# A cross-network kernel (CIN) with x1 split by one instruction per chunk into two buffers, and 31 rounded fields in the last layer

## The chip, the cores and the metric

The kernel runs on one core of a Trainium2 chip. The metric is device time in microseconds, from the first to the last instruction with what lies around it. Engines are named as in the profile: PE is TensorE (matmuls; PEld is its weight load), DVE is VectorE, ACT is ScalarE, POOL is GpSimd, SP is SyncE, which here only issues DMAs.

## The reference

512 samples, 39 embedded fields of 16 dimensions. Three "cross" layers, whose outputs are summed over the 16 dimensions, and a small MLP behind them:

```python
def _cin_layer(X0, Xi, W, b):          # X0: [512, 39, 16], Xi: [512, fields, 16]
    Wr = W.reshape(H, F0_, Fi)
    return jnp.einsum('hjk,bjd,bkd->bhd', Wr, X0, Xi) + b[None, :, None]
Xi = X0
for W, b in Ws:                        # 3 layers of 128 outputs each
    Xi = _cin_layer(X0, Xi, W, b)
    res.append(Xi.sum(axis=2))
z = jnp.concatenate(res, axis=1)       # [512, 384]
h = jnp.concatenate([z, dense_ctx], axis=1)
h = jnp.maximum(h @ W_top1 + b_top1, 0.0)
h = jnp.maximum(h @ W_top2 + b_top2, 0.0)
y = h @ W_top3
```

## The kernel before

**Tiling.** The 512 samples go through in 16 chunks of 32 samples, so a chunk is 512 columns (sample times dimension), and a chunk in 4 groups of 128 columns. Rows of the tables are gathered by GpSimd three chunks ahead, laid out by a transpose, written to a scratch in DRAM and read back in the layouts that the layers need.

**Layer 0** of the next chunk is 7 fp32 matmuls (`layer0`, L409) into the PSUM bank `acc0`, each on a product that GpSimd makes (`multiply0`, L259). They are spread through the current chunk by a list written by hand (`L0_AFTER`, L75), the last one behind block 1 of group 3. Then `evacuate_x1` (L655, ScalarE) writes `x1` = `acc0` + bias. The columns of `acc0` are interleaved by group, so the read steps over four fp32 values at a time, and `x1` lies group after group.

**Layer 1** needs `x1` as two values that the fast matmul form (fp32r, 3 matmuls for one product) takes: `x1h`, `x1` rounded by a ScalarE copy, and `x1l` = `x1` - `x1h`, by VectorE. There is one buffer of each. To let the next chunk's values be written while group 3 of the old one is still being used, both are made in two pieces: FRONT, the 384 columns of groups 0 to 2 (ScalarE L662, VectorE L577 by `split_x1`), and BACK, the 128 columns of group 3 (ScalarE L667 in `split_back`, VectorE L577), which is made early in the chunk itself, once the last matmuls of the old chunk are through. TensorE waits for the first at group 0 (L445) and for the second at group 3 (L447).

A group of layer 1 is 10 blocks (`layer1_block`, L424) of 3 matmuls L436 to L438, 4 fields (512 columns) to a block. Each block's output is multiplied with `x0t` and summed by its owner, `OWNERS = "ADADAADADA"` (L59): six blocks go to ScalarE (banks `ya`, four), which scales them into `prods`, and four (numbers 1, 3, 6 and 8) to VectorE (banks `yd`, two), which chains multiply-adds (L558). VectorE also adds up `prods` in two halves per group (`sum_half`, L561, L573) into `x2t`. TensorE may write block 3 of a group into its `yd` bank only when VectorE is through with block 8 of the group before.

**Order on VectorE at the turn between chunks** (`chunk`, L585): multiply-adds of block 6 of group 3; FRONT of the next x1; the sum of half 0; the multiply-adds of block 8; then in the next chunk those of block 1; BACK; the sum of half 1, on which the `gram_group` matmul (L416) waits; block 3. One chunk later in the order, at group 1, `sum_dims` (L580) sums `x1` over the dimensions. Chunks 1 to 14 are a hardware loop on VectorE and chunks 1 to 13 on ScalarE; TensorE's are written out.

**Last layer** (L505): 39 fields of `w2` times `gram` into one bank. The first `whole` = 12 fields are plain fp32 matmuls (L509); the last `split` = 27 take three fp32r matmuls each (L514 to L518). For these, `w2` is split into the space of `w1h`/`w1l` (23 fields) and then of `x1h`/`x1l` (4 fields, 512 columns) by ScalarE L729 and VectorE L627, and each field of `gram` by ScalarE L735 and VectorE L632, through a ring of four. ScalarE evacuates the last `gram` group (L671) behind its two `w2` pieces.

Of the kernel before, what the change touches and what calls it, by code (L numbers as in the profile page):

```python
# [119 lines left out]
def build(nc, a):  # L120
    ctx = ExitStack()
    with ctx:
        def sb(name, shape, dt=F32):
            return ctx.enter_context(nc.sbuf_tensor(name, shape, dt))
# [4 lines left out]
        def sem(name):  # L129
            return ctx.enter_context(nc.semaphore(name))  # L130
# [17 lines left out]
        x1h = sb("x1h", [P, COLS], F32R)  # L148
        x1l = sb("x1l", [P, COLS], F32R)
# [6 lines left out]
        z = sb("z", [P, 2, B])  # L156
# [20 lines left out]
        split = near + COLS // H  # L177
        whole = F - split

        def w2_halves(i):  # L180
# [4 lines left out]
            return x1h[:, cols], x1l[:, cols]  # L185
# [5 lines left out]
        def w2_pieces():  # L191

            rows = w2[:, whole:F, :].rearrange("p j h -> p (j h)")
            return ((rows[:, 0:near * H], w1h[:, first_split * H:], w1l[:, first_split * H:]),
                    (rows[:, near * H:], x1h[:, :], x1l[:, :]))

        h1, h2 = gram[:, 0:4, :], gram[:, 4:6, :]
# [25 lines left out]
        x1h_front, x1h_back = sem("x1h_front"), sem("x1h_back")  # L223
        x1_front, x1_back = sem("x1_front"), sem("x1_back")
# [8 lines left out]

        FRONT, BACK = slice(0, (GROUPS - 1) * P), slice((GROUPS - 1) * P, COLS)
# [39 lines left out]
        def _(sp):  # L274
# [48 lines left out]
            sp.wait_ge(x1_back, CHUNKS)  # L323
# [69 lines left out]
        def _(pe):  # L393
# [30 lines left out]
            def layer1_block(n, g, q):  # L424
# [12 lines left out]
                pe.matmul(out, x1h[:, xs], w1l[:, cols], start=False, stop=False)  # L437
                pe.matmul(out, x1l[:, xs], w1h[:, cols], start=False, stop=True).then_inc(ready, 1)  # L438

            def chunk(c, prev, nxt, lay):  # L440

                l0_after = L0_AFTER if prev else L0_AFTER_0
                for g in range(GROUPS):
                    if g == 0:
                        pe.wait_ge(x1_front, c + 1)  # L445
                    if g == GROUPS - 1:
                        pe.wait_ge(x1_back, c + 1)  # L447
                    for q in range(BLOCKS):
                        layer1_block(GROUPS * c + g, g, q)
# [39 lines left out]
            def hidden1_early(m):  # L489
                pe.matmul(hid[m][:, :], wt1_0[:, m * P:(m + 1) * P], z[:, 0, :], start=True, stop=False)  # L490
# [33 lines left out]
            for m, out in enumerate(hid):  # L524
                pe.matmul(out[:, :], wt1[:, 1, m * P:(m + 1) * P], z[:, 1, :],
                          start=False, stop=True).then_inc(tail_mm, 1)
# [14 lines left out]
        def _(dve):  # L541
# [33 lines left out]
            def split_x1(c, cols, high, done):  # L575
                dve.wait_ge(high, c + 1)
                dve.tensor_tensor(x1l[:, cols], x1[:, cols], x1h[:, cols].bitcast(F32),  # L577
                                  ALU.subtract).then_inc(done, 1)

            def sum_dims(c):  # L580
                dve.tensor_reduce(z[:, 0, bass.ds(c * CB, CB)].rearrange("p (g b) -> p g b", g=GROUPS),
                                  x1[:, :].rearrange("p (g d b) -> p g b d", g=GROUPS, d=D), AX.X,
                                  ALU.add).then_inc(z_sums, 1)
# [34 lines left out]
            split_x1(0, FRONT, x1h_front, x1_front)  # L618
# [16 lines left out]
        def _(act):  # L635
# [19 lines left out]
            def evacuate_x1(c):  # L655
# [31 lines left out]
            def chunk(c, prev, nxt, lay):  # L687
                split_back(c)
# [50 lines left out]
            act.activation(z[:, 1, :], yd[0][:, :], ACT.Identity, bias=bias2d[:, 0:1]).then_inc(tail_act, 1)  # L739
# [74 lines left out]
```

## Time and profile before

| what | value |
|---|---|
| median of 3 runs | 677.56 us (677.14 to 682.29) |
| the profiled execution | 677.52 us |
| its span, first to last instruction | 675.7 us |
| TensorE, busy share | 95% |
| VectorE, busy share | 85% |
| ScalarE, busy share | 76% |
| GpSimd, busy share | 51% |

Busy time of TensorE is a union of pipelined matmuls whose ends are modelled: a 512-column fp32r matmul is shown with 0.39 us, but one starts every 0.227 us. So the distance between starts is what is read on TensorE, and a gap shows as a start that comes later than that. The same holds in part for VectorE and ScalarE, where the next instruction may start a little before the shown end of the one before.

### The profile page before, as it was taken

The numbers are of one execution on the slowest core, as the hardware profiler recorded it, in microseconds if no ns is written. First come the engines' busy times: TensorE is split into PE (matmuls) and PEld (weight loads), VectorE is DVE, ScalarE is ACT, GpSimd is POOL, SyncE is SP. The second block draws the span as 40 slices with busy tenths as digits, with TensorE's granted clock in tenths as the row PEclk, the third lists the DMA queues.
The fourth block names the chain that finished last, engine by engine and source line by source line (L and its number), as shares of the span: only waits on it lengthen the run. The fifth ranks groups of instructions, "written<-read, shape, count | busy, mean of one in ns | idle before, by whom it ended". The sixth has DMA issues, their size and how long they took to land.

```text
span 675.7 us, 13663 instructions
## 1 busy us (share of the span) xinstructions
PE 639.8 (95%) x2489; PEld 457.9 (68%) x2489; DVE 577.4 (85%) x1240; ACT 514.3 (76%) x1676; POOL 346.7 (51%) x339
## 2 busy tenths in 40 slices
PE   0389999999999999999999999999999999999998
PEld 0166677677777777777777777777777777766473
DVE  0457898989899999989998989999999989999580
ACT  2156878888787878787878878787878887899372
POOL 6778384838474665647383847475563333220000
PEclk9989999999999999999999999999999999999999
DMA  6532723232231303131323222231313130000200
GB/s 220 137 101 57 242 65 90 53 88 53 63 78 49 93 22 91 32 97 44 88 53 89 52 73 68 56 85 30 86 29 105 31 102 16 13 16 2 62 1 0
DMA packets 42542, 46.12 MB, mean 68 GB/s; under 512 B 20704, under 2 KB 25408, under 8 KB 42377
## 3 DMA queue, kind: packets, MB, share of 16 engines
q1 hardware_dynamic: 26146, 42.28, 21.3%
q0 software_dynamic: 5120, 1.32, 2.1%
q10 hardware_dynamic: 11239, 2.05, 1.7%
q8 instruction: 20, 0.33, 0.2%
q14 instruction: 17, 0.14, 0.1%
HBM read 44.30 MB, written 1.31 MB: 68 GB/s over the span
## 4 chain that ended last, share of the span: by engine, by line
PE 82%; POOL 4%; DVE 4%; issue 4%; DMA 3%; SPq 1%; ACT 1%; DVEq 0%; ACTq 0%; POOLq 0%
PE acc L413 14%; PE ya L436 11%; PE ya L437 11%; PE ya L438 10%; PE yd L436 8%; PE yd L438 7%; PE yd L437 7%; PE misc L420 4%; POOL emb L339 3%; DVE chain L558 2%; DMA tiles<-x_rows 2%; PE yd L509 2%; POOL prod L266 1%; PE yd L514 1%; PE yd L518 1%
## 5 line engine op out<-in xcount | busy, mean ns | idle before, releaser
L683 ACT ACTIVATE prods<-ya,x0t 128x128 f32<-128x128 f32 x1472 | 442.5, 501 | 100.5 <-PE ya L438 100.1
L558 DVE SCALAR_TENSOR_TENSOR chain<-yd,x0t,chain 128x128 f32<-128x128 f32 x768 | 218.2, 343 | 14.4 <-PE yd L438 13.7
L436 PE MATMUL ya<-w1h,x1h 128*128 128x512 f32 (+1 forms) x384 | 206.4, 537 | 1.9 <-DVE x1l L577 1.9
L266 POOL TENSOR_TENSOR prod<-tiles,x0a 120x512 f32<-120x512 f32 x105 | 137.3, 1308 | 126.7 <-PE acc L413 113.0
L339 POOL DMA_INDIRECT emb<-in_tables,rows x160 | 159.1, 994 | 39.4 <-issue 26.1
L437 PE MATMUL ya<-w1l,x1h 128*128 128x512 f32 (+1 forms) x384 | 148.3, 386 | 0.0
L438 PE MATMUL ya<-w1h,x1l 128*128 128x512 f32 (+1 forms) x384 | 147.7, 385 | 0.0
L573 DVE TENSOR_REDUCE x2t<-prods 128x128 f32<-128x1792 f32 x64 | 129.2, 2019 | 1.5 <-DVE chain L558 0.3
L413 PE MATMUL acc<-prod,w 120*128 120x512 f32 x224 | 117.3, 608 | 10.6 <-DVE prod L266 8.8
L573 DVE TENSOR_REDUCE prods<-prods 128x128 f32<-128x1536 f32 x64 | 111.7, 1745 | 0.0
L436 PE MATMUL yd<-w1h,x1h 128*128 128x512 f32 x256 | 104.2, 407 | 1.7 <-DVE chain L558 0.7
L438 PE MATMUL yd<-w1h,x1l 128*128 128x512 f32 x256 | 101.1, 395 | 0.0
L437 PE MATMUL yd<-w1l,x1h 128*128 128x512 f32 x256 | 100.5, 392 | 0.0
L436 PEld LDWEIGHTS ya<-w1h,x1h 128*128 128x128 f32 x384 | 72.3, 188 | 38.1 <-issue 25.8
L437 PEld LDWEIGHTS ya<-w1l,x1h 128*128 128x128 f32 x384 | 72.7, 189 | 35.1 <-issue 24.3
L350 POOL TENSOR_TENSOR diag<-x0t,const 128x320 f32<-128x320 f32 x64 | 46.4, 724 | 93.0 <-PE misc L420 92.9
L438 PEld LDWEIGHTS ya<-w1h,x1l 128*128 128x128 f32 x384 | 72.3, 188 | 14.0
L436 PEld LDWEIGHTS yd<-w1h,x1h 128*128 128x128 f32 x256 | 48.3, 189 | 25.8 <-DVE prods L558 8.0
L413 PEld LDWEIGHTS acc<-prod,w 120*128 120x128 f32 x224 | 42.4, 193 | 25.7 <-issue 9.8
L438 PEld LDWEIGHTS yd<-w1h,x1l 128*128 128x128 f32 x256 | 48.2, 188 | 10.4
L437 PEld LDWEIGHTS yd<-w1l,x1h 128*128 128x128 f32 x256 | 48.2, 188 | 10.2 <-issue 0.5
L558 DVE SCALAR_TENSOR_TENSOR prods<-yd,x0t,chain 128x128 f32<-128x128 f32 x128 | 47.0, 464 | 0.0
(87 smaller groups left out, 409.0 us busy)
## 6 DMA issues: line engine op xcount, KB each, us to landing
tiles<-x_rows SPq DMA_DIRECT2D x236, 78.0 KB
x0a<-x_rows SPq DMA_DIRECT2D x45, 80.0 KB
emb<-in_tables,rows POOLq DMA_INDIRECT x160, 2.5
w<-in_w SPq DMA_DIRECT2D x3, 832.0 KB, 10.5
w<-in_w SPq DMA_DIRECT2D x1, 2496.0 KB, 11.4
tiles<-x_rows SPq DMA_DIRECT2D x32, 42.0 KB
x<-x_rows SPq DMA_DIRECT2D x16, 78.0 KB
x<-x_rows SPq DMA_DIRECT2D x16, 77.8 KB
```

Source lines behind the costliest of these rows:

```text
L266: engine.tensor_tensor(prod0[:, i % L0_PRODS, :], tiles[:, slot, :], x0a[:, :], ALU.mult).then_inc(prod0_ready, 1)
L339: pool.indirect_dma_start(emb[:, c % 2, fo * D:(fo + 1) * D], None, a["tables"], bass.IndirectOffsetOnAxis(ap=rows[:, c, fo:fo + 1].bitcas ...
L350: pool.tensor_tensor(diag[:, n % 2, :, :], row.to_broadcast([P, GB, F1]), mask.to_broadcast([P, GB, F1]), ALU.mult).then_inc(diag_ready, 1)
L413: pe.matmul(acc0[:, :], w0[:, i, :], prod0[:, i % L0_PRODS, :], start=(i == 0), stop=(i == T0 - 1)).then_inc(l0_done, 1)
L420: pe.matmul(misc[:, 0:GB * F1], x2t[:, g, :], diag[:, g % 2, :, :].rearrange("p b j -> p (b j)"), start=True, stop=True).then_inc(g_done, 1)
L436: pe.matmul(out, x1h[:, xs], w1h[:, cols], start=True, stop=False)
L437: pe.matmul(out, x1h[:, xs], w1l[:, cols], start=False, stop=False)
L438: pe.matmul(out, x1l[:, xs], w1h[:, cols], start=False, stop=True).then_inc(ready, 1)
L509: pe.matmul(l2[:, :], w2[:, j, :], gram[:, j, :], start=(j == 0), stop=False)
L558: dve.scalar_tensor_tensor(out, product, x, run if step else b1[:, :], ALU.mult, ALU.add).then_inc(yd_used, 1)
L573: dve.tensor_reduce(out, src, AX.X, ALU.add).then_inc(sums_done, 1)
L683: mm = act.activation(prods[:, :, slot_of(q) + i], ya[(NA * g + k) % YA][:, i * H:(i + 1) * H], ACT.Copy, scale=turned(c)[:, g * F1 + j:g ...
```

## The change

`x1h` and `x1l` get two buffers each, used by even and odd chunks. ScalarE rounds all 512 columns of `x1` in one instruction in `evacuate_x1`; `split_back` is gone. VectorE makes all 512 columns of `x1l` in one instruction, where FRONT was made; it now reads `acc0` itself, adds the bias and subtracts `x1h`. The BACK instruction and its wait are gone, and TensorE waits once per chunk, at group 0. The space of the second buffers also takes four more fields of `w2`, so 31 fields of the last layer are split (three fp32r matmuls) and 8 stay whole. `z` loses its second half, whose place a free row of `gram` takes. The diff, with the waits of SyncE and what only renames left out:

```diff
-        x1h = sb("x1h", [P, COLS], F32R)
-        x1l = sb("x1l", [P, COLS], F32R)
+        x1h = sb("x1h", [P, 2, COLS], F32R)
+        x1l = sb("x1l", [P, 2, COLS], F32R)
...
-        split = near + COLS // H
+        split = near + 2 * COLS // H
         whole = F - split
...
-        h1, h2 = gram[:, 0:4, :], gram[:, 4:6, :]
+        h1, h2, z1 = gram[:, 0:4, :], gram[:, 4:6, :], gram[:, 6, :]
...
-                pe.matmul(out, x1h[:, xs], w1h[:, cols], start=True, stop=False)
+                pe.matmul(out, x1h[:, c % 2, xs], w1h[:, cols], start=True, stop=False)
...
                     if g == 0:
-                        pe.wait_ge(x1_front, c + 1)
-                    if g == GROUPS - 1:
-                        pe.wait_ge(x1_back, c + 1)
+                        pe.wait_ge(x1_split, c + 1)
...
-            def split_x1(c, cols, high, done):
-                dve.wait_ge(high, c + 1)
-                dve.tensor_tensor(x1l[:, cols], x1[:, cols], x1h[:, cols].bitcast(F32),
-                                  ALU.subtract).then_inc(done, 1)
+            def halves(x, c):
+                return x[:, bass.ds(c & 1, 1), :].rearrange("p c (g n) -> p (c g) n", n=P)
+
+            def split_x1(c):
+
+                dve.wait_ge(x1h_ready, c + 1)
+                dve.scalar_tensor_tensor(halves(x1l, c), acc0[:, :].rearrange("p (n g) -> p g n", g=GROUPS), bias[:, 0:1],
+                                         halves(x1h, c).bitcast(F32), ALU.add, ALU.subtract).then_inc(x1_split, 1)
...
                             if nxt and (g, half) == (GROUPS - 1, 1):
-                                split_x1(c + 1, FRONT, x1h_front, x1_front)
-                            if (g, half) == (0, 0):
-                                split_x1(c, BACK, x1h_back, x1_back)
+                                split_x1(c + 1)
...
                 act.wait_ge(x1_ready, c + 1)
-                act.activation(x1h[:, FRONT], x1[:, FRONT], ACT.Copy).then_inc(x1h_front, 1)
-
-            def split_back(c):
-
-                wait_done(act, ya_ready, NA * GROUPS * c)
-                act.activation(x1h[:, BACK], x1[:, BACK], ACT.Copy).then_inc(x1h_back, 1)
+                act.activation(x1h[:, bass.ds(c & 1, 1), :].rearrange("p c n -> p (c n)"), x1[:, :],
+                               ACT.Copy).then_inc(x1h_ready, 1)
...
             def chunk(c, prev, nxt, lay):
-                split_back(c)
```

## Rows read from the trace of the kernel before

**Rows 1.** the page: busy time of each engine, share of the span, instructions
```profile
PE 639.8 (95%) x2489; PEld 457.9 (68%) x2489; DVE 577.4 (85%) x1240; ACT 514.3 (76%) x1676; POOL 346.7 (51%) x339
```

**Rows 2.** busy us of each engine in chunks 1 to 14 and the last
```profile
96.00:592.00 496.00, 495.50 (x1985) 364.26 (x1984) 463.54 (x1023) 408.00 (x1386) 274.85 (x265) 1.00 0.24 62
592.00:624.00 32.00, 30.73 (x125) 22.43 (x124) 32.00 (x74) 29.44 (x98) 4.73 (x5) 1.00 0.03 9
```

**Rows 3.** waits: TensorE on x1l, us in total, times, longest us
```profile
PE ya L436 <- DVE x1l L577: 1.9, 1, 1.9
```

**Rows 4.** VectorE's timeline at a turn: start us, us, what, idle before
```profile
298.19 0.55 DVE L577 TENSOR_TENSOR x1l<-x,x1h 128x384 fp32r<-128x384 f32 x1
298.65 1.75 DVE L573 TENSOR_REDUCE prods<-prods 128x128 f32<-128x1536 f32 x1
...
300.83 0.74 DVE L558 SCALAR_TENSOR_TENSOR prods<-yd,x0t,chain 128x128 f32<-128x128 f32 x2
301.88 0.35 DVE L558 SCALAR_TENSOR_TENSOR chain<-yd,x0t,b 128x128 f32<-128x128 f32 x1 [0.30 <-DVE prods L558]
...
302.92 0.28 DVE L577 TENSOR_TENSOR x1l<-x,x1h 128x128 fp32r<-128x128 f32 x1
...
310.48 0.35 DVE L558 SCALAR_TENSOR_TENSOR chain<-yd,x0t,b 128x128 f32<-128x128 f32 x1 [0.36 <-PE yd L438]
```

**Rows 5.** timeline of TensorE over the same turn
```profile
299.20 0.39 PE L436 MATMUL ya<-w1h,x1h 128*128 128x512 f32 x1
...
301.27 0.40 PE L438 MATMUL ya<-w1h,x1l 128*128 128x512 f32 x1
301.63 0.50 PE L436 MATMUL yd<-w1h,x1h 128*128 128x512 f32 x1
```

**Rows 6.** TensorE at the first and the last of such turns
```profile
119.19 0.50 PE L436 MATMUL yd<-w1h,x1h 128*128 128x512 f32 x1
...
592.77 0.50 PE L436 MATMUL yd<-w1h,x1h 128*128 128x512 f32 x1 [0.16 <-DVE prods L558]
```

**Rows 7.** groups by shape: count, busy us, mean ns, idle us before
```profile
L558 DVE SCALAR_TENSOR_TENSOR chain<-yd,x0t,chain 128x128 f32<-128x128 f32 x768 | 218.2, 343 | 14.4 <-PE yd L438 13.7
...
L573 DVE TENSOR_REDUCE prods<-prods 128x128 f32<-128x1536 f32 x64 | 111.7, 1745 | 0.0
...
L632 DVE TENSOR_TENSOR w1l<-gram,w1h 128x512 fp32r<-128x512 f32 x27 | 18.2, 692 | 7.3 <-PE yd L518 7.3
...
L581 DVE TENSOR_REDUCE z<-x 128x512 f32 x14 | 16.3, 1161 | 0.0
L659 ACT ACTIVATE x<-acc,bias 128x512 f32<-128x512 f32 x16 | 11.0, 688 | 6.3 <-PE acc L413 6.3
...
L662 ACT ACTIVATE x1h<-x 128x384 fp32r<-128x384 f32 x16 | 8.4, 526 | 0.5
...
L729 ACT ACTIVATE w1h<-w 128x2944 fp32r<-128x2944 f32 x1 | 2.7, 2690 | 0.0
...
L746 ACT ACTIVATE gram<-yd,bt 128x512 f32<-128x512 f32 x1 | 0.7, 687 | 2.7 <-PE yd L531 2.7
...
L729 ACT ACTIVATE x1h<-w 128x512 fp32r<-128x512 f32 x1 | 0.6, 629 | 0.0
```

**Rows 8.** timeline of TensorE at the end of the last layer
```profile
654.76 0.39 PE L514 MATMUL yd<-w1h,x1h 128*128 128x512 f32 x1
...
657.48 1.02 PE L522 MATMUL acc<-gram,prods 128*128 128x512 f32 x2
...
660.91 1.02 PE L525 MATMUL acc<-z,prods 128*128 128x512 f32 x2
```

**Rows 9.** timeline of ScalarE ahead of the last layer
```profile
628.13 0.44 ACT L671 ACTIVATE gram<-misc 128x320 f32<-128x320 f32 x1 [0.86 <-PE misc L420]
```

**Rows 10.** timeline of VectorE ahead of the last layer
```profile
630.88 2.49 DVE L632 TENSOR_TENSOR w1l<-gram,w1h 128x512 fp32r<-128x512 f32 x4
```

**Rows 11.** timeline of TensorE after the turn into chunk 1
```profile
83.12 1.12 PE L413 MATMUL acc<-prod,w 120*128 120x512 f32 x2 [0.25 <-POOL prod L266]
```

More of the change, by code:

```diff
@@ L155, in build @@
         gram = sb("gram", [P, F1, B])
-        z = sb("z", [P, 2, B])
+        z = sb("z", [P, B])
         wt3 = sb("wt3", [P, HID2 // P])
@@ L176, in build, with flat @@
         near = F - first_split
-        split = near + COLS // H
+        split = near + 2 * COLS // H
         whole = F - split
+        def flat(x):
+            return x[:, :, :].rearrange("p i n -> p (i n)")
         def w2_halves(i):
@@ L184, in w2_halves @@
             cols = slice((i - near) * H, (i - near + 1) * H)
-            return x1h[:, cols], x1l[:, cols]
+            return flat(x1h)[:, cols], flat(x1l)[:, cols]
         def gram_halves(i):
@@ L194, in w2_pieces @@
             return ((rows[:, 0:near * H], w1h[:, first_split * H:], w1l[:, first_split * H:]),
-                    (rows[:, near * H:], x1h[:, :], x1l[:, :]))
-        h1, h2 = gram[:, 0:4, :], gram[:, 4:6, :]
+                    (rows[:, near * H:], flat(x1h), flat(x1l)))
+        h1, h2, z1 = gram[:, 0:4, :], gram[:, 4:6, :], gram[:, 6, :]
         scratch = nc.dram_tensor("x0_rows", (CHUNKS, FP, COLS), F32, kind="Internal").ap()
@@ L222, in build @@
         x1_ready = sem("x1_ready")
-        x1h_front, x1h_back = sem("x1h_front"), sem("x1h_back")
-        x1_front, x1_back = sem("x1_front"), sem("x1_back")
+        x1h_ready, x1_split = sem("x1h_ready"), sem("x1_split")
         z_sums = sem("z_sums")
@@ L232, in build @@
         tail_mm, tail_act = sem("tail_mm"), sem("tail_act")
-        FRONT, BACK = slice(0, (GROUPS - 1) * P), slice((GROUPS - 1) * P, COLS)
         def chunk_rows(c):
@@ L322, in _ @@
                 sp.dma_start(tiles[row:row + DENSE, 0, :], a["dense_t"]).then_inc(dense_in, 16)
-            sp.wait_ge(x1_back, CHUNKS)
+            sp.wait_ge(x1_split, CHUNKS)
             sp.wait_ge(z_sums, CHUNKS)
@@ L422, in gram_group, with layer1_block @@
                           start=True, stop=True).then_inc(g_done, 1)
-            def layer1_block(n, g, q):
+            def layer1_block(c, g, q):
+                n = GROUPS * c + g
                 k = OWNERS[:q].count(OWNERS[q])
@@ L435, in layer1_block @@
                 xs, out = slice(g * P, (g + 1) * P), out[:, 0:len(fields) * H]
-                pe.matmul(out, x1h[:, xs], w1h[:, cols], start=True, stop=False)
-                pe.matmul(out, x1h[:, xs], w1l[:, cols], start=False, stop=False)
-                pe.matmul(out, x1l[:, xs], w1h[:, cols], start=False, stop=True).then_inc(ready, 1)
+                pe.matmul(out, x1h[:, c % 2, xs], w1h[:, cols], start=True, stop=False)
+                pe.matmul(out, x1h[:, c % 2, xs], w1l[:, cols], start=False, stop=False)
+                pe.matmul(out, x1l[:, c % 2, xs], w1h[:, cols], start=False, stop=True).then_inc(ready, 1)
             def chunk(c, prev, nxt, lay):
@@ L444, in chunk @@
                     if g == 0:
-                        pe.wait_ge(x1_front, c + 1)
-                    if g == GROUPS - 1:
-                        pe.wait_ge(x1_back, c + 1)
+                        pe.wait_ge(x1_split, c + 1)
                     for q in range(BLOCKS):
-                        layer1_block(GROUPS * c + g, g, q)
+                        layer1_block(c, g, q)
                         if nxt and (g, q) in l0_after:
@@ L489, in hidden1_early @@
             def hidden1_early(m):
-                pe.matmul(hid[m][:, :], wt1_0[:, m * P:(m + 1) * P], z[:, 0, :], start=True, stop=False)
+                pe.matmul(hid[m][:, :], wt1_0[:, m * P:(m + 1) * P], z[:, :], start=True, stop=False)
             pe.wait_ge(mlp0_in, 16)
@@ L524, in _ @@
             for m, out in enumerate(hid):
-                pe.matmul(out[:, :], wt1[:, 1, m * P:(m + 1) * P], z[:, 1, :],
+                pe.matmul(out[:, :], wt1[:, 1, m * P:(m + 1) * P], z1,
                           start=False, stop=True).then_inc(tail_mm, 1)
@@ L573, in sum_half @@
                 dve.tensor_reduce(out, src, AX.X, ALU.add).then_inc(sums_done, 1)
[L575 to L578 removed]
+            def halves(x, c):
[4 more added lines that the diff above has]
+                                         halves(x1h, c).bitcast(F32), ALU.add, ALU.subtract).then_inc(x1_split, 1)
             def sum_dims(c):
[L581 removed]
+                dve.tensor_reduce(z[:, bass.ds(c * CB, CB)].rearrange("p (g b) -> p g b", g=GROUPS),
                                   x1[:, :].rearrange("p (g d b) -> p g b d", g=GROUPS, d=D), AX.X,
@@ L617, in _ @@
             dve.wait_ge(bias_in, 3 * 16)
-            split_x1(0, FRONT, x1h_front, x1_front)
+            split_x1(0)
             chunk(0, False, True)
@@ L738, in _ @@
             act.wait_ge(bias2d_ready, 1)
-            act.activation(z[:, 1, :], yd[0][:, :], ACT.Identity, bias=bias2d[:, 0:1]).then_inc(tail_act, 1)
+            act.activation(z1, yd[0][:, :], ACT.Identity, bias=bias2d[:, 0:1]).then_inc(tail_act, 1)
             act.wait_ge(mlp_in, 5 * 16)
```

## The prediction

> **What bounds the kernel now.** I read the page first: TensorE is busy 95% of the span [rows 1]. The busy time by stretch then says where another engine counts. In chunks 1 to 14, 496 of 676 us, TensorE is busy all the time, VectorE 93%, ScalarE 82%; in the last chunk, which has no layer 0 to compute, it is VectorE that is busy for 32.00 of 32.00 us [rows 2]. The waits are next: TensorE waited for `x1l` once in the whole run, 1.9 us before chunk 0, and never for it at a later chunk nor at group 3 [rows 3]. So the second buffers take away no wait, since there is none, and the question is what the re-cut instructions do to the order on VectorE.
>
> The timelines of VectorE and TensorE at a turn between chunks answer where that order reaches TensorE. From the multiply-adds of block 6 VectorE goes on without a pause through FRONT (start 298.19), the sum of half 0 (298.65) and block 8, whose last instruction ends at 300.83 + 0.74 = 301.57 [rows 4]. TensorE's block 3 of the new chunk needs that bank. The matmul ahead of it starts at 301.27, so it could start at 301.27 + 0.23 = 301.50; it starts at 301.63, 0.06 after VectorE's end, and without its weights loaded ahead, so its second matmul comes 0.1 late too [rows 5]. This stall recurs at all 14 turns into chunks 2 to 15, from 119.19 us to 592.77 [rows 6]. It is short, about 0.24 us, but it means that at each turn TensorE is released by VectorE: whatever VectorE does more between blocks 6 and 8 is paid in full.
>
> **The split on VectorE.** FRONT takes 0.46 us of VectorE from start to start (298.65 - 298.19), 0.09 less than its shown 0.55 [rows 4]. In its place comes one scalar_tensor_tensor of 512 columns from PSUM. No row shows it. The nearest: the subtraction of 512 SBUF columns is shown with 0.692 us, and scalar_tensor_tensor of 128 columns from PSUM with 0.343 [rows 7], against 0.28 for the 128-column subtraction in SBUF [rows 4]. So PSUM and the third operand add 0.06, and the estimate is 0.75 shown, 0.75 - 0.09 = 0.66 from start to start: 0.20 us more than FRONT. The lower bound is the SBUF row alone, 0.60 from start to start, 0.14 more. 
>
> BACK (0.28 shown, 0.25 from start to start) goes, but it comes after block 1 of the new chunk, behind the release of TensorE [rows 4]. It gives VectorE slack there, and VectorE has some already: at group 1 it waits 0.36 us for TensorE [rows 4]. Worth nothing in chunks 1 to 14. In the last chunk VectorE is the bound, and there it counts: 0.20 - 0.25 = -0.05 us.
>
> The sum over turns: 13 turns, into chunks 2 to 14, by 0.20 = +2.6 us. The turn into chunk 1 I take as free: behind it TensorE waits 0.25 us for a product from GpSimd [rows 11], which swallows 0.20. The last turn: -0.05.
>
> **TensorE at the start of a chunk.** The merged wait stands at group 0. TensorE's first matmul is at 299.20, its weight load (which reads `x1h`, so the wait stands before it) about 0.17 earlier [rows 5]. The new instruction ends at 298.19 + 0.75 = 298.94, some 0.06 later it is seen. That is just in time. Should it be late by up to 0.2 or 0.3, TensorE would only wait there and not at block 3, which VectorE releases anyway. So nothing is added. Queued behind this wait is all of TensorE, but the later stall covers it.
>
> **ScalarE.** In the loop the rounding grows from 0.526 to about 0.629 [rows 7] and the BACK copy goes: ScalarE, busy 82%, gains, and nobody waits for it. Ahead of chunk 0 the longer copy stands before the layout of chunk 1, whose DMAs feed GpSimd's first products, which pace the start: 0.629 - 0.526 = +0.1 us.
>
> **The last layer.** Four fields go from one fp32 matmul to three fp32r ones. Twelve of the latter, four fields, take 657.48 - 654.76 = 2.72 us, 0.68 a field; four fp32 matmuls of 512 columns take 660.91 - 657.48 = 3.43, 0.86 each [rows 8]. Saved: 3.43 - 2.72 = 0.71 us. What has to be ready: ScalarE's second weight piece is 1024 columns, +512 at (2.690 - 0.629) / 2432 = 0.85 ns each, [rows 7], +0.43 us ahead of the last `gram` evacuation; that one idles 0.86 us now [rows 9], so it stays hidden, and without that cover it would delay the whole layer by 0.43. VectorE's piece grows by about 0.53 us (its four first low parts, which begin at 630.88 and take 2.49, end at 633.9) [rows 10]; TensorE comes to the first rounded field after 8 whole ones, at about 635.6. Hidden too. The ring keeps its pace, four more fields of 0.68 us against 0.60 on VectorE.
>
> **The sum** against the profiled run (span 675.7, 677.52 with what lies around it; the median is 677.56, the same): +2.6 - 0.05 + 0.1 - 0.71 = +1.9, that is **679.5 us**. With the lower bound, 13 x 0.14, it is 678.7; with 0.1 of sequencer work in each turn, 680.9.
>
> **Rivals.** *The step over PSUM costs (the other side: slower).* The new instruction reads `acc0` at every fourth value. The one VectorE row with a read of large step is the sum over dimensions, stepping over eight values in SBUF: 1.161 us for 512 elements [rows 7]. The dense sums take 1.745 for 1536 [rows 7]; at the 1.07 ns an element of the subtractions ((0.692 - 0.28) / 384) 512 would take 0.65. So a step can cost 0.51 us, one ns an element. If PSUM at step four behaves so, the instruction takes 0.75 + 0.51 = 1.26, and each turn costs 0.71 instead of 0.20: 13 x 0.71 = 9.2, the last turn +0.46, the turn into chunk 1 about +0.46, +0.1, -0.71: +9.5, **687.0 us**. It decides from 1.08 us on: then 14 x 0.53 = 7.4 less 0.6 is the 1% of 677.5. Against it: ScalarE reads `acc0` with the same step in 0.688, and dense PSUM columns in 0.687 [rows 7]: no cost there. But that is another engine. The Trainium skill (SBUF — State Buffer, under Door 1: The DMA port swizzle) speaks for it: lines are 16 bytes in SBUF and 8 in PSUM, and each access that crosses to a new one pays. By that rule every one of the 512 reads pays, and the time is this rival's; ScalarE's row disagrees with it, the sum over dimensions agrees. Chance 0.16.
>
> *The longer instruction is hidden.* If TensorE is not released by that bank but by something that stays, or if the new instruction overlaps its neighbours so that it takes no more than FRONT, only the other terms are left: -0.71 + 0.1 - 0.25 = -0.9, **676.7 us**. For it: the stall is small, 0.13 us before the matmul, and one instruction replaces two. Against it: the matmul starts 0.06 us behind VectorE's end at all 14 turns. Chance 0.13.
>
> *The change doesn't do what it says*: as a removal of waits for the old buffer it does nothing here, which is inside the forecast. What is left, 0.05, is a start-up that moves by other waits, to either side.
>
> **How the numbers follow.** Forecast 0.66 (679.5, own range 678.7 to 680.9), step cost 0.16 (687.0), hidden 0.13 (676.7), other 0.05. The forecast alone holds less than 8 in 10, and the unknown cost has its upper bound at 687; so the range goes from 676.4 to 687.2. About 1% (6.8 us) is what a measurement of this kernel can tell from no change. Forecast and hidden lie within it: 0.79. Slower by more: the step cost and 0.02 of the rest, 0.18. Faster by more: 0.03, since the largest gain that any row offers is 0.9 us.
>
> **What would show it.** The new instruction's row: 0.75 us is the forecast, 1.1 and more the step cost, 0.69 the lower bound. The first matmul of block 3 at each turn: its gap grows from 0.13 to about 0.33, and it starts 0.06 behind the last multiply-add of block 8. The turns lie (301.63 - 119.19) / 5 = 36.49 us apart now by the same matmul [rows 5, 6]; 36.69 is expected. The last layer: 8 whole and 31 split fields, 0.71 us shorter from first to last. No wait of TensorE for `x1l` longer than 0.3 at a turn. I am wrong if the new instruction takes what I say and the turns don't lengthen (then VectorE's bank was not what released TensorE), or if ScalarE's pieces push the last `gram` evacuation.

## The result and the profile after

The changed kernel takes 682.11 us (median of 15 runs, 680.94 to 683.25) against 677.76 for the kernel before in the same comparison: a ratio of 1.0062 with an interval of 1.0052 to 1.0072. That is 4.35 us more, inside the 1% that was forecast as "no change" and inside the range of 676.4 to 687.2, but slower than the likeliest case: +1.9 us was predicted, and the forecast's own range ended at 680.9. The profiled spans say the same, 680.0 against 675.7, +4.3.

The page of the kernel after, its first lines, answers [rows 1]:

```profile
span 680.0 us, 13680 instructions
PE 638.1 (94%) x2493; PEld 458.6 (67%) x2493; DVE 582.8 (86%) x1228; ACT 518.1 (76%) x1664; POOL 343.7 (51%) x339
```

The bound has not moved to another engine. VectorE is busy for 5.4 us more than before, but 3.3 of them lie behind layer 1, where four more fields are split, and TensorE is busy for 1.7 us less. So the 4.3 us must be places at which TensorE stands still. The same stretches as in [rows 2] (columns: window, length, busy time and instructions of each engine), in the kernel after:

```profile
96.00:595.00 499.00, 494.48 (x1979) 363.22 (x1978) 464.38 (x1008) 408.15 (x1369) 273.13 (x266) 1.00 0.24 62
595.00:628.00 33.00, 31.54 (x132) 23.61 (x131) 33.00 (x75) 30.31 (x102) 4.73 (x5) 1.00 0.03 9
```

VectorE is again busy throughout the last chunk, and TensorE, by its modelled ends, nearly throughout the loop. So neither view finds the loss; the waits do. The list of TensorE's waits in the kernel after, two of its lines, to lay beside [rows 3] (us together, times, longest):

```profile
PE yd L437 <- DVE prods L557: 4.1, 15, 0.5
PE ya L437 <- DVE x1l L580: 2.2, 1, 2.2
```

The first line is the one that changed: `yd` for VectorE's last multiply-adds, 15 times, 4.1 us together (before it was 0.6 us in 3). `x1l` is waited for once, before chunk 0, and never at a later turn.

VectorE at the turn that [rows 4] show, kernel after:

```profile
298.33 2.28 DVE L557 SCALAR_TENSOR_TENSOR chain<-yd,x0t,chain 128x128 f32<-128x128 f32 x8
300.62 0.75 DVE L580 SCALAR_TENSOR_TENSOR x1l<-acc,bias,x1h 128x512 f32 x1
301.29 1.75 DVE L572 TENSOR_REDUCE prods<-prods 128x128 f32<-128x1536 f32 x1
302.95 0.60 DVE L557 SCALAR_TENSOR_TENSOR chain<-yd,x0t,chain 128x128 f32<-128x128 f32 x2
303.46 0.72 DVE L557 SCALAR_TENSOR_TENSOR prods<-yd,x0t,chain 128x128 f32<-128x128 f32 x2
```

and TensorE there, for [rows 5]:

```profile
303.62 0.40 PE L439 MATMUL ya<-w1h,x1l 128*128 128x512 f32 x1
304.23 0.50 PE L437 MATMUL yd<-w1h,x1h 128*128 128x512 f32 x1 [0.22 <-DVE prods L557]
```

Three things are to be read. The new instruction is shown with 0.75 us and takes 301.29 - 300.62 = 0.67 from start to start. It starts 0.01 after the shown end of the multiply-add ahead of it (298.33 + 2.28 = 300.61), where one usually starts 0.09 before that end. And block 3 starts at 304.23, 0.05 after VectorE's end (303.46 + 0.72 = 304.18), when it could have started at 303.62 + 0.23 = 303.85: a gap of 0.38 where it was 0.13.

Where the 4.3 us lie, from the starts of TensorE's 640 blocks of layer 1 in both traces:

| stretch | before, us | after, us | difference |
|---|---|---|---|
| start of the program to the first block of chunk 2 | 116.62 | 117.51 | +0.9 |
| chunks 2 to 14, first block to first block | 473.74 | 477.81 | +4.07 (13 x 0.31) |
| chunk 15, first block to last | 31.96 | 32.02 | +0.06 |
| last block to the end (last layer, MLP) | 53.40 | 52.67 | -0.73 |

Inside a chunk, the median distances between the starts of neighbouring blocks differ by more than 0.015 us in two places alone: from block 2 to block 3 of group 0, the turn, +0.28 us, and from block 7 to block 8 of group 1, +0.07. Together that is 0.04 more than the chunk's 0.31; the rest is spread over distances that differ by less. The first row of the table is to be taken with care: in the traces of the kernels of this document the same stretch ends anywhere from 114.1 to 117.5 us.

The last layer, TensorE, kernel after, for [rows 8]: the last fp32r matmuls on `x1h`/`x1l` and the first of what follows.

```profile
656.33 0.39 PE L513 MATMUL yd<-w1h,x1h 128*128 128x512 f32 x1
...
661.54 0.39 PE L517 MATMUL yd<-w1l,x1h 128*128 128x512 f32 x1
661.77 1.02 PE L521 MATMUL acc<-gram,prods 128*128 128x512 f32 x2
```

Eight fields of three matmuls in 661.77 - 656.33 = 5.44 us, 0.68 a field, as forecast. And ScalarE ahead of it, for [rows 9]:

```profile
631.65 1.07 ACT L725 ACTIVATE x1h<-w 128x1024 fp32r<-128x1024 f32 x1
633.14 0.44 ACT L668 ACTIVATE gram<-misc 128x320 f32<-128x320 f32 x1 [0.42 <-PE misc L420]
```

Its idle time before the last `gram` went from 0.86 to 0.42: the longer piece is hidden, with 0.42 to spare.

### The profile page after: what moved, and what is told of

It reads as the page before. It is cut to its first block, busy times and chain, and to the rows that moved or that the text cites. A ratio compares the mean times of both kernels' runs of the same rounds, so it can differ in the third digit from the quotient of the medians.

```text
span 680.0 us, 13680 instructions
## 1 busy us (share of the span) xinstructions
PE 638.1 (94%) x2493; PEld 458.6 (67%) x2493; DVE 582.8 (86%) x1228; ACT 518.1 (76%) x1664; POOL 343.7 (51%) x339
## 4 chain that ended last, share of the span: by engine, by line
PE 65%; issue 12%; DVE 11%; POOL 5%; DMA 2%; DVEq 2%; SPq 1%; ACT 0%; ACTq 0%; POOLq 0%
PE acc L413 11%; PE ya L437 8%; PE ya L438 8%; PE ya L439 8%; PE yd L437 7%; PE yd L439 6%; PE yd L438 6%; DVE chain L557 5%; PE misc L420 3%; POOL emb L339 3%; DVE z L584 2%; DVE prods L557 1%; POOL prod L266 1%; PE yd L508 1%; PE yd L513 1%
## 5 line engine op out<-in xcount | busy, mean ns | idle before, releaser
L339 POOL DMA_INDIRECT emb<-in_tables,rows x160 | 156.7, 979 | 39.4 <-issue 33.9
```

The costliest lines, as they stand in the source:

```text
L339: pool.indirect_dma_start(emb[:, c % 2, fo * D:(fo + 1) * D], None, a["tables"], bass.IndirectOffsetOnAxis(ap=rows[:, c, fo:fo + 1].bitcas ...
```

## Experiments

The theory after the result: **the turn pays in full** for what VectorE does between block 6 and block 8, and that is now 0.20 for the longer instruction plus about 0.1 of sequencer work. The rivals: the time comes from the PSUM operand or its step; from the other half of the change (the split fields, or work moved away from behind the turn); or it is not paid at the turn at all.

### Work added ahead of the awaited block, and behind it

To the kernel before, one 128-column subtraction into a tile that nobody reads, right behind FRONT (it takes 0.20 us from start to start, what the new instruction was forecast to add):

```diff
+            def more():
+                dve.tensor_tensor(junk[:, :], x1[:, 0:P], x1h[:, 0:P].bitcast(F32), ALU.subtract)
...
                                 split_x1(c + 1, FRONT, x1h_front, x1_front)
+                                more()
```

> The kernel before with one more VectorE subtraction of 128 columns (0.25 us from start to start) into a scratch tile that nobody reads, right behind FRONT, so between blocks 6 and 8 at every turn. Theory (VectorE's order at the turn releases TensorE, each us there is paid in full): turn period 36.49 + 0.25 = 36.74 us, 13 turns x 0.25 + 0.25 in the last chunk = +3.5 us, about 681.3. Rival (TensorE's small gap at the turn has another cause, VectorE has slack): no change, 677.7.

Measured: 681.81 us, ratio 1.0073 (1.0055 to 1.0091); span 679.4. VectorE at the turn in this kernel:

```profile
259.21 2.27 DVE L559 SCALAR_TENSOR_TENSOR chain<-yd,x0t,chain 128x128 f32<-128x128 f32 x8
261.40 0.55 DVE L578 TENSOR_TENSOR x1l<-x,x1h 128x384 fp32r<-128x384 f32 x1
261.87 0.28 DVE L582 TENSOR_TENSOR junk<-x,x1h 128x128 fp32r<-128x128 f32 x1
262.07 1.75 DVE L574 TENSOR_REDUCE prods<-prods 128x128 f32<-128x1536 f32 x1
```

The 0.20 us put in there lengthen the distance from block 2 to block 3 by 0.18 and the chunk by 0.18 (36.66 us; 36.74 was expected, with 0.25 put in), 13 x 0.18 = 2.3 us. The rest of its loss is something else: at two turns, 1.1 us each, shown further down.

The same instruction, ahead of the sum of half 0 at group 0 instead:

```diff
+                            if (g, half) == (0, 1):
+                                more()
```

> The kernel before with the same additional 128-column subtraction, once per chunk, but behind block 6 of group 0, where VectorE has 0.36 us of slack later on (it waits for TensorE at group 1). Theory (only the place between blocks 6 and 8 of group 3 counts): turn period stays 36.49, +0.25 us in the last chunk alone, 678.0. Rival (it is VectorE's total load or shared memory traffic that costs, wherever the work stands): the same +3.5 us as with the work ahead.

Measured: 677.69 us, ratio 1.0006 (0.9994 to 1.0018), chunks unchanged at 36.48 us. The same work is free 9 us later in the order. So the turn pays in full, and it is the place that costs, not the work.

### The remainder out of SBUF instead of out of the bank

From the kernel after, with `x1` from SBUF in place of `acc0` and the bias; everything else stays:

```diff
-                dve.scalar_tensor_tensor(halves(x1l, c), acc0[:, :].rearrange("p (n g) -> p g n", g=GROUPS), bias[:, 0:1],
-                                         halves(x1h, c).bitcast(F32), ALU.add, ALU.subtract).then_inc(x1_split, 1)
+                dve.tensor_tensor(halves(x1l, c), x1[:, :].rearrange("p (g n) -> p g n", n=P), halves(x1h, c).bitcast(F32),
+                                  ALU.subtract).then_inc(x1_split, 1)
```

> The changed kernel, its one instruction per chunk reading x1 from SBUF (a tensor_tensor of 512 columns) instead of the layer-0 bank plus bias; addresses still by register. Theory (instruction 0.06 shorter; the pause of 0.10 ahead of it is the sequencer's register work and stays): turn period 36.79 - 0.06 = 36.73, 13 x 0.06 = 0.8 us less than the changed kernel, 681.3. Rival (the pause belongs to the third operand and the read from PSUM): pause gone too, 36.63, 2.1 us less.

Measured: 680.73 us, ratio 1.0062 (1.0041 to 1.0084). VectorE at its turn:

```profile
331.50 2.28 DVE L557 SCALAR_TENSOR_TENSOR chain<-yd,x0t,chain 128x128 f32<-128x128 f32 x8
333.78 0.69 DVE L580 TENSOR_TENSOR x1l<-x,x1h 128x512 f32 x1
334.39 1.75 DVE L572 TENSOR_REDUCE prods<-prods 128x128 f32<-128x1536 f32 x1
```

The instruction is 0.06 shorter (0.61 from start to start), and the turn is 0.06 shorter than in the kernel after, 0.21 over the kernel before. The time can't tell these two kernels apart, and one turn of this trace lost 1.1 us for another reason, shown further down. But the pause ahead of it is the same: it again starts at the shown end of the multiply-add (331.50 + 2.28 = 333.78), not 0.09 before. So the pause is not PSUM's, nor the third operand's. What both kernels have is the address that hangs on the chunk. The line of the new instruction in the kernel after (durations in ns, minimum, median, maximum):

```profile
L580 DVEq ALU_OP  x28: 40/42/45, 116.4 to 594.2; - x28
L580 DVE SCALAR_TENSOR_TENSOR x1l<-acc,bias,x1h x16: 745/751/751, 38.7 to 594.4; 128x512 f32 x14, 128x512 fp32r<-128x512 f32 x2
L580 DVEq FUSED_REGOPS  x14: 75/75/75, 116.6 to 594.3; - x14
```

VectorE's sequencer (DVEq) executes three register instructions of this line, besides one for the wait, at each of the 14 turns whose chunk number is a register.

### Fixed addresses

From the kernel after: VectorE's loop takes two chunks a pass, so that the buffer is a constant in the code.

```diff
-            with dve.Fori(1, CHUNKS - 1) as c:
-                chunk(c, True, True)
-            chunk(CHUNKS - 1, True, False)
+            with dve.Fori(1, CHUNKS - 1, 2) as c:
+                chunk(c, True, True, 1)
+                chunk(c + 1, True, True, 0)
+            chunk(CHUNKS - 1, True, False, 1)
```

> The changed kernel, VectorE's loop taking two chunks per pass, so that the buffer's address is fixed in the instruction. Theory (the 0.10 us pause ahead of the new instruction in the loop is sequencer register work): pause gone, turn period 36.79 - 0.10 = 36.69, 1.3 us less than the changed kernel, 680.8; the extra 0.06 at the group-1 sum over dimensions may go too (another 0.7). Rival (the pause belongs to the instruction's operands): period stays 36.79 and the time 682.1.

Measured: 702.14 us, ratio 1.0352 (1.0315 to 1.0389). As a way to a faster kernel this failed, for a reason of its own, but on the pause it is clear. The line of the new instruction now has no register instructions:

```profile
L580 DVE SCALAR_TENSOR_TENSOR x1l<-acc,bias,x1h x16: 740/742/750, 39.2 to 616.4; 128x512 fp32r<-128x512 f32 x16
```

VectorE's timeline at a turn inside a pass of the same kernel:

```profile
346.16 2.18 DVE L557 SCALAR_TENSOR_TENSOR chain<-yd,x0t,chain 128x128 f32<-128x128 f32 x8
348.25 0.74 DVE L580 SCALAR_TENSOR_TENSOR x1l<-acc,bias,x1h 128x512 fp32r<-128x512 f32 x1
```

It starts 0.09 before the shown end of the multiply-add (346.16 + 2.18 = 348.34): the pause of 0.1 is gone, with the bank and its step still read. That the turn itself got no shorter (5.83 to 5.88 us from block 6 to block 3, 5.84 in the kernel after) is because another pause grew earlier: at the turns inside a pass the sum ahead of block 6's multiply-adds starts 0.68 us behind the multiply-add before it, where it is 0.42 in the kernel after, with no further register instruction on record. So the 0.1 can't be priced by this kernel's time.

Most of the loss comes at the loop's branch. The chain of waits there:

```profile
311.78 0.04 DVEq L621
311.82 0.10 DVE prods L557
311.92 2.79 issue
314.70 0.07 DVEq L621
```

and VectorE's timeline:

```profile
315.13 0.35 DVE L557 SCALAR_TENSOR_TENSOR chain<-yd,x0t,b 128x128 f32<-128x128 f32 x1 [2.89 <-issue]
```

Between two instructions of the loop's own line, L621, the sequencer shows nothing for 2.9 us, with nothing awaited, and the chunks with the branch are 41.0 to 41.1 us long in four passes and 39.5 to 39.6 in two, instead of 36.8 for the others. The 1.5 us between the four and the two are TensorE's clock. Behind each branch TensorE waits twice, for 0.7 to 0.9 and then for 1.2 us, and in those four passes, and in no other chunk of layer 1, the granted clock is 0.50 (1.2 GHz) for 3.4 us. The first of the four stretches (the third figure from the end is the granted clock):

```profile
162.60:166.00 3.40, 3.24 (x7) 2.49 (x8) 3.40 (x10) 1.69 (x6) 1.53 (x2) 0.50 0.47 143
```

So without the clock a chunk with the branch is 2.7 to 2.8 us longer. Of the two queues that load instructions one moved as many packets as before, the other 18 in the kernel after, by the queue part of its page,

```profile
q14 instruction: 18, 0.14, 0.1%
```

and 55 here:

```profile
q14 instruction: 55, 0.45, 0.2%
```

Only VectorE's program differs, so that queue is taken for VectorE's, and it loads instructions again while the loop runs. A pass is 250 of VectorE's recorded instructions in the kernel after and 492 here. The Trainium skill (Runtime: NRT & Kernel Launch, under Instruction fetch mechanics) has a rule that fits: instructions are held in two blocks of 256, and a taken branch to a target outside them waits for a fetch. The traces agree in direction: a pass of 250 can lie within two blocks, one of 492 hardly can. The length was not varied further, so that it decides is likely and not shown.

### What of the pause a plain subtraction shows

From the kernel before, with FRONT's address through a register, `(c & 0)` for its buffer:

```diff
+            def by_register(x, c, cols):
+                return x[:, bass.ds(c & 0, 1), :].rearrange("p c n -> p (c n)")[:, cols]
```

> The kernel before, where FRONT's two buffer addresses come from a register (chunk number and 0, so always the same buffer) instead of standing in the instruction; same operands, same size, same place. Theory (the pause of 0.10 ahead of the changed kernel's new instruction is the sequencer's address arithmetic): in the loop FRONT starts 0.35 instead of 0.26 us after the multiply-add ahead of it, the turn period grows by about 0.09, 36.49 to 36.57, 13 x 0.09 = +1.2 us. Rival (the pause belongs to the operand from PSUM or the third operand): no pause, 36.48, same time as before.

Measured: 676.85 us, ratio 1.0002 (0.9991 to 1.0013), turns as before. This tells nothing: the expression was folded into a constant when the program was built, and the trace has no register instructions for it.

So again, with two real buffers for FRONT and one for BACK:

```diff
+            def buffer_of(x, c, cols):
+                return x[:, bass.ds(c & 1, 1), :].rearrange("p c n -> p (c n)")[:, cols]
...
+                if cols is FRONT:
+                    dve.tensor_tensor(buffer_of(x1l2, c, cols), x1[:, cols], buffer_of(x1h2, c, cols).bitcast(F32),
+                                      ALU.subtract).then_inc(done, 1)
+                    return
```

> The kernel before, where FRONT (384 columns, both operands in SBUF, same place) goes to one of two buffers by the chunk's number, so that VectorE's addresses are computed in registers: two more sequencer instructions ahead of it than before, one less than in the changed kernel. (The run front_by_register was meant to show this, but the address was folded into the instruction.) Theory (the pause of 0.10 ahead of the changed kernel's new instruction is the sequencer's address arithmetic): FRONT starts 0.31 to 0.35 instead of 0.26 us after the multiply-add ahead of it in the loop and the turn period grows by the same 0.05 to 0.09, 36.53 to 36.58, about +0.9 us. Rival (the pause belongs to the operand from PSUM or the third operand): 0.26, 36.48, same time as before.

Measured: 678.08 us, ratio 1.0011 (0.9993 to 1.0029). The turn grew by 0.03, not by the 0.05 to 0.09 that I expected. Here two register instructions come between the multiply-add and FRONT, not three. The start of FRONT is 0.28 behind that of the multiply-add; it is 0.26 without them and 0.35 to 0.36 with three (the kernel after and the one out of SBUF). So the sequencer's work is not simply added: about two such instructions fit beside the running multiply-add, and the third shows with 0.07 to 0.08.

### The other half of the change alone

The kernel before with 31 split fields in the last layer (and the space and the place of `z` that they need), its FRONT and BACK as they were:

```diff
-        split = near + COLS // H
+        split = near + 2 * COLS // H
```

> The kernel before with nothing but the last layer's part of the change: 31 fields rounded, 8 whole, the additional space a second buffer that layer 1 doesn't use. Theory (the last layer is TensorE's alone and its two preparations stay hidden): -0.71 us, from the last block of chunk 15 to the end 52.69 instead of 53.40 us; the turn period stays 36.49; about 676.7. Rival (the longer weight pieces on ScalarE and VectorE eat it): tail 53.1 or more.

Measured: 676.54 us, ratio 0.9986 (0.9976 to 0.9996), span 674.3; from the last block to the end 52.68 us, 0.72 less than before, and chunks of 36.45 us. The fields give what was forecast, and nothing else hangs on them.

### Less ahead of the awaited block

If the turn pays in full, it must also gain. From the kernel before, FRONT is cut to the 128 columns of group 0, which is all that TensorE needs first, and BACK gets the other 384, behind the turn:

```diff
-        FRONT, BACK = slice(0, (GROUPS - 1) * P), slice((GROUPS - 1) * P, COLS)
+        FRONT, BACK = slice(0, P), slice(P, COLS)
...
-                    if g == GROUPS - 1:
+                    if g == 1:
                         pe.wait_ge(x1_back, c + 1)
...
-                            if (g, half) == (0, 0):
+                            if (g, half) == (0, 1):
                                 split_x1(c, BACK, x1h_back, x1_back)
```

> The kernel before with the cut moved: FRONT is group 0 alone (128 columns), BACK is groups 1 to 3 (384), subtracted behind block 6 of group 0, and TensorE waits for it at group 1. One buffer, fixed addresses. Theory (VectorE's work between blocks 6 and 8 is what TensorE waits for at the turn): 0.46 - 0.25 = 0.21 us less there, gap before block 3 nearly gone, turn period 36.49 - 0.2 = 36.29, 13 turns = -2.7 us, about 674.5 against 677.5. Rival (the later BACK uses up VectorE's 0.36 us of slack at group 1, or meets GpSimd's reads): the stall at block 8 of group 1 grows by what block 3 wins, 677.5.

Measured: 674.12 us, ratio 0.9947 (0.9934 to 0.9961). The chunk is 0.24 us shorter, 0.13 from block 2 to 3 and 0.11 from block 3 to 4. With the 31 fields as well:

```diff
-        split = near + COLS // H
+        split = near + 2 * COLS // H
```

> front_one and the 31 rounded fields together. Theory (both gains are in different stretches and add): -2.7 - 0.7 = -3.4 us, about 674. Rival: as for the two alone, 676.8.

Measured: 673.09 us, ratio 0.9934 (0.9921 to 0.9947). VectorE and TensorE at a turn of this kernel:

```profile
330.05 2.27 DVE L562 SCALAR_TENSOR_TENSOR chain<-yd,x0t,chain 128x128 f32<-128x128 f32 x8
332.23 0.28 DVE L581 TENSOR_TENSOR x1l<-x,x1h 128x128 fp32r<-128x128 f32 x1
332.44 1.74 DVE L577 TENSOR_REDUCE prods<-prods 128x128 f32<-128x1536 f32 x1
```

```profile
335.32 0.40 PE L442 MATMUL ya<-w1h,x1l 128*128 128x512 f32 x1
335.55 0.40 PE L440 MATMUL yd<-w1h,x1h 128*128 128x512 f32 x1
335.79 0.40 PE L441 MATMUL yd<-w1l,x1h 128*128 128x512 f32 x1
```

Block 3 starts 0.23 us after the matmul ahead of it, and its second matmul 0.24 later: the stall is gone, and with it the 0.1 us that a matmul lost whose weights had not been loaded ahead.

From the kernel after, its two buffers kept, with only group 0's 128 columns of the remainder at the old place and the rest in group 0:

```diff
-                                split_x1(c + 1)
+                                split_x1(c + 1, slice(0, P), x1_split)
+                            if (g, half) == (0, 1):
+                                split_x1(c, slice(P, COLS), x1_rest)
```

> The changed kernel (two buffers, one ScalarE rounding, 31 fields), VectorE's subtraction from SBUF cut in two: group 0 ahead, groups 1 to 3 behind block 6 of the chunk's group 0, all addresses by register. Theory: ahead stand 0.25 + 0.10 of register work = 0.35 instead of 0.77 in the changed kernel and 0.46 before: turn period 36.49 - 0.11 + 0.06 (register work near the sum over dimensions) = 36.44, tail -0.7, about 676.3; so 1.5 to 2 us behind front_one_31. Rival (register work doesn't matter once it is off the new instruction): same as front_one_31.

Measured: 675.28 us, ratio 0.9963 (0.9950 to 0.9976). The turn has no stall here either, and the chunk is 36.29 us, 0.15 shorter than expected: with the stall gone, the register work at the turn is no longer paid (block 6 to block 3 takes 5.44 us here and in the kernel without it). The 0.06 us before block 8 of group 1 stay, and they are also in the kernel out of SBUF (0.07), but not in the one with FRONT in two buffers. So the length of the new instruction is not their cause.

### The same reading at the next stall

With the turn free, the stall that is left is before block 8 of group 1, 0.28 us in the kernel before (a gap of 0.17 before its first matmul, at 315.78, and 0.11 more before its second): the sum over the dimensions (1.16 us on VectorE) stands ahead of the multiply-adds that free the bank. Moved from group 1 to half 1 of group 2, on top of the kernel with the 128-column FRONT and 31 fields:

```diff
-                            if (g, half) == (1, 0):
+                            if (g, half) == (2, 1):
                                 sum_dims(c)
```

> front_one_31, with VectorE's sum over dimensions (1.06 us from start to start) moved from block 1 of group 1 to block 6 of group 2, ahead of VectorE's longest idle time in a chunk (0.78 us before group 3). Theory (what stands on VectorE ahead of a bank that TensorE waits for is paid, work ahead of idle time is not): the stall before block 8 of group 1 (0.43 - 0.23 that a preceding layer-0 or gram matmul explains = 0.2) goes, turn period 36.23 - 0.25 = about 36.0, another 3 us, about 670. Rival (group 2 has no room: VectorE is late for block 3 of group 3 by what it wins): period stays 36.2, 673.

Measured: 669.42 us, ratio 0.9887 (0.9869 to 0.9905). This is the best version. The chunk is 35.96 us, 0.52 less than before: 0.22 at the turn and 0.28 at blocks 7 to 9 of group 1. VectorE at the sum's new place, group 2: it waits 0.66 us for TensorE before the multiply-adds of block 6 (second line), and the sum follows the one of half 0:

```profile
355.74 1.12 DVE L562 SCALAR_TENSOR_TENSOR chain<-yd,x0t,chain 128x128 f32<-128x128 f32 x4
357.52 1.13 DVE L562 SCALAR_TENSOR_TENSOR chain<-yd,x0t,chain 128x128 f32<-128x128 f32 x4 [0.66 <-PE yd L442]
358.56 1.74 DVE L577 TENSOR_REDUCE prods<-prods 128x128 f32<-128x1536 f32 x1
360.22 1.12 DVE L585 TENSOR_REDUCE z<-x 128x512 f32 x1
```

That move alone, on the kernel before:

```diff
-                            if (g, half) == (1, 0):
+                            if (g, half) == (2, 1):
                                 sum_dims(c)
```

> The kernel before with nothing but the sum over dimensions moved to block 6 of group 2. Theory (its cost is the stall before block 8 of group 1, independent of the turn): period 36.49 - 0.25 = 36.24, 14 chunks = -3.5 us, about 673.5. Rival (it only paid because front_one had freed VectorE at the turn): less than 1 us.

Measured: 674.11 us, ratio 0.9950 (0.9934 to 0.9966), 0.24 us a chunk: 0.28 less at blocks 7 to 9 of group 1, 0.05 more at the turn, which is still in the way here. The two add up: 0.9950 and the 0.9934 of the kernel with the short FRONT and 31 fields multiply to 0.9884, where 0.9887 was measured.

## Why the prediction was right in kind and short in size

The mechanism was right, the sum was not complete. 682.1 lies 1.2 us outside the 678.7 to 680.9 that the forecast gave itself, and within the full range only because that had to reach up to a rival, the step over PSUM, that did not come true. The terms one by one:

- **What bounds the kernel**: right. TensorE is held by VectorE's last multiply-adds at each turn, and both signs show there: 0.20 us more on VectorE lengthens the chunk by 0.18, and 0.25 less takes the whole stall away, 0.24. The same work behind the turn is free.
- **The new instruction**: right. 0.751 us shown, 0.67 from start to start, 0.20 more than FRONT; forecast 0.75 and 0.66.
- **The sequencer's work**: wrong, and the term that was mis-sized first. I took nothing and allowed 0.1; it is 0.1. The reasoning was that inside a block it lies beside a running instruction. That holds only for what fits beside it, here a multiply-add of 0.26 us from start to start, and three register instructions and the wait do not.
- **The turn as a whole**: +0.28, against 0.20. Its pieces on VectorE, 0.20 and 0.10, make 0.30, and TensorE follows 0.05 instead of 0.06 behind. The gap is 0.38 where about 0.33 was to be seen, and the turns lie 36.79 us apart instead of 36.69.
- **Block 8 of group 1**: not forecast, +0.07 a chunk, 0.9 us in all by itself. It arises 4 us earlier, where two multiply-adds take 0.67 from their start to the next instruction instead of 0.58 (lines below, kernel after). The recorded instructions there are the same in both kernels, but between two register instructions of the sequencer 0.22 us pass instead of 0.13. In the kernel with the short first piece and two buffers such a pause stands two instructions earlier; in the one with two chunks a pass four such pauses, of 0.3 to 0.4 us, stand at the pass's recorded VectorE instructions 72, 201, 327 and 456, that is 126 to 129 apart, and the kernel after has the first two, of 0.1 us, at the same numbers (the kernel before has one of 0.1 at 200). So they seem to go with the place in the code and not with what the instruction does. What makes them is open.

```profile
313.60 0.67 DVE L557 SCALAR_TENSOR_TENSOR chain<-yd,x0t,chain 128x128 f32<-128x128 f32 x2
314.27 2.02 DVE L572 TENSOR_REDUCE x2t<-prods 128x128 f32<-128x1792 f32 x1
```

- **The last turn and chunk**: forecast -0.05 (0.20 - 0.25), measured +0.06. Block 3 comes 0.30 later and 0.23 are won back at block 7, where BACK is gone, so this is the 0.1 of the sequencer again.
- **The start**: forecast +0.1, measured +0.9, open. The turn into chunk 1, taken as free, has 0.12 of it (block 2 to block 3). From the first block of chunk 0 to that of chunk 2 it takes 76.8 us before and 77.9 after. In kernels whose start is the same as before's it scatters from 75.9 to 76.9, and in the three others with the changed start it is 75.9, 76.7 and 77.0. TensorE waits 1.5 us for ScalarE in chunk 0 of the kernel after, and in no other of these. A stretch of 3.4 us at a granted clock of 0.50 stands in chunk 0 of the kernel before as well as of the kernel after. So the traces don't show this 0.9 as the change's. The medians are 4.35 us apart (3.5 to 4.9 by the interval), and the other rows of the table give 3.4, so something may be left for it; no run isolates it.
- **The last layer**: right, -0.73 against -0.71, and ScalarE's idle time shrank by 0.44 where 0.43 was computed.
- **TensorE at the start of a chunk**: right. No wait for `x1l` at any later turn.
- **The rivals**: *the step over PSUM costs* is refuted for VectorE: 0.751 with the step of four, where the estimate without any cost was 0.75, and 0.06 more than the dense subtraction in SBUF, for the step, the bank and the third operand together. The rule of the Trainium skill that spoke for it (SBUF — State Buffer, under Door 1: The DMA port swizzle) does not show in this instruction. *Hidden* is refuted by the kernels with work added and taken away at the turn.

By the terms: measured less forecast is 4.3 - 1.9 = 2.4 us. Chunks 2 to 14 hold 4.07 - 2.6 = 1.5 of it (13 x 0.08 = 1.0 at the turn, 13 x 0.07 = 0.9 at block 8, and 0.04 a chunk the other way in differences too small to place), the last chunk 0.1, the start 0.8, the last layer nothing. So of the sum the sequencer's term, put at nothing, was the one that the runs explain; block 8 of group 1 and the start stay open.

## What to carry to other kernels

At a point where the bound engine is already released by another, everything ahead of the release costs its full length, and gains it back until the wait is gone: ask of each instruction there whether it is needed there, and put the rest where its engine has idle time (here 128 of 384 columns were needed, and a sum that nobody awaits stood ahead of a bank; 0.5% each). Merging two instructions into one is no gain when the merged one is on the path and the removed one was not. An operand whose address comes from a loop register costs sequencer instructions in front of the engine's instruction: count them against the instruction that runs meanwhile.

## What the runs showed of the hardware

- **VectorE's register work hides beside the running instruction only in part.** Starts 0.26 us apart with none, 0.28 with two, 0.35 to 0.36 with three, at 40 to 75 ns each.
- **A loop body of about 490 instructions on VectorE cost 2.7 to 2.8 us a pass**, seen as one pause of 2.8 behind the branch (311.92), and 1.5 more in four passes of six, in which TensorE's granted clock was 0.50 for 3.4 us behind its waits; a body of 250 shows no such pause.
- **VectorE's sequencer pauses at places some 128 recorded instructions apart**, for about 0.1 us in the loop of 250 instructions and 0.3 to 0.4 us in the one of 492. The cause is not shown.
- **GpSimd and a subtraction of two SBUF operands on VectorE block each other.** Their timelines at one turn of the kernel before:

```profile
553.49 0.55 DVE L577 TENSOR_TENSOR x1l<-x,x1h 128x384 fp32r<-128x384 f32 x1
553.58 1.61 POOL L266 TENSOR_TENSOR prod<-tiles,x0a 120x512 f32<-120x512 f32 x1
```

of the kernel that takes the remainder out of SBUF:

```profile
554.19 1.84 DVE L580 TENSOR_TENSOR x1l<-x,x1h 128x512 f32 x1
554.20 1.29 POOL L266 TENSOR_TENSOR prod<-tiles,x0a 120x512 f32<-120x512 f32 x1
```

and of the kernel after:

```profile
521.36 1.30 POOL L266 TENSOR_TENSOR prod<-tiles,x0a 120x512 f32<-120x512 f32 x1
521.37 0.75 DVE L580 SCALAR_TENSOR_TENSOR x1l<-acc,bias,x1h 128x512 f32 x1
```

In the first pair (the subtraction started first) GpSimd's product takes 1.61 instead of 1.30; in the second, started within 0.01 us of each other, it is the subtraction that takes 1.84 instead of 0.69, 1.15 more. In the third, with the bank as one operand, both keep their time. The two events of 1.1 us in the kernel with work added ahead are of this kind:

```profile
555.80 1.62 POOL L267 TENSOR_TENSOR prod<-tiles,x0a 120x512 f32<-120x512 f32 x1
556.18 1.39 DVE L582 TENSOR_TENSOR junk<-x,x1h 128x128 fp32r<-128x128 f32 x1
```

The Trainium skill (SBUF — State Buffer, under Who interferes with whom) states this: a VectorE instruction with two SBUF inputs contends with a GpSimd instruction that reads SBUF, and issue order decides who is held. These pairs agree on the contention; that issue order decides is seen in the first and the last, while in the second the starts are too close to tell. The kernel after had none of it in its trace, as its instruction reads only one of its two tensors from SBUF; the forecast did not count that.
